# Layer normalisation of the first attention layer moved from VectorE to ScalarE, from the third batch on

## What is computed

```
def _layernorm(x, axis=-1, eps=1e-05):
    m = jnp.mean(x, axis=axis, keepdims=True)
    v = jnp.var(x, axis=axis, keepdims=True)
    return (x - m) / jnp.sqrt(v + eps)
...
    x = x + _L0_attn_a_ref(_layernorm(x, axis=-1), ...)
    x = x + _L0_ffn_ref(_layernorm(x, axis=-1), ...)
    x = x + _L0_attn_b_ref(_layernorm(x, axis=-1), ...)
    x = x + _L0_ffn_ref(_layernorm(x, axis=-1), ...)
```

## Time and profile before

| what | value |
|---|---|
| median of 3 runs | 965.94 us (963.97 to 966.96) |
| the profiled execution's own time | 966.79 us |
| its span, first to last instruction | 965.1 us |
| busy: PE, DVE, ACT, POOL | 890.3, 733.7, 533.5, 381.6 us |
| mean granted TensorE clock | 0.975 |

### The profile page before, as it was taken

One profiled execution on the slowest core, in us unless ns is written; L12 is line 12 of the kernel. 1 busy time (PEld: TensorE's weight loads), 2 busy tenths in 40 slices (PEclk: granted clock), 3 DMA queues, 4 the chain that ended last, 5 costly groups with the idle time before them and its releaser, 6 DMA issues.

```text
span 965.1 us, 20229 instructions
## 1 busy us (share of the span) xinstructions
PE 890.3 (92%) x6766; PEld 696.7 (72%) x6766; DVE 733.7 (76%) x2379; ACT 533.5 (55%) x1410; POOL 381.6 (40%) x554
## 2 busy tenths in 40 slices
PE   5779998989999999978999999999999997999996
PEld 4656776767767776656878888788878776777763
DVE  6668888889889887664766767685867677889973
ACT  6545454543445454526667575757575762554555
POOL 2468788876535443351212112020202000444445
PEclk9789999999999999989999999999999999999999
DMA  6432333331113655001202020202112021132321
GB/s 199 61 54 56 54 45 55 54 55 36 35 35 68 134 109 132 2 16 41 45 1 45 1 44 2 45 2 45 23 23 45 1 34 33 38 62 47 73 48 35
DMA packets 51287, 46.63 MB, mean 48 GB/s; under 512 B 6624, under 2 KB 48624, under 8 KB 51184
## 3 DMA queue, kind: packets, MB, share of 16 engines
q1 hardware_dynamic: 51184, 45.34, 23.4%
HBM read 11.40 MB, written 2.10 MB: 14 GB/s over the span
## 4 chain that ended last, share of the span: by engine, by line
PE 35%; DVE 12%; issue 4%; ACT 1%; DMA 1%; POOL 0%; SPq 0%; POOLq 0%; ACTq 0%; DVEq 0%
PE bank L285 9%; PE bank L1928 5%; PE bank L1878 5%; PE bank L1936 4%; PE bank L1866 3%; DVE weights L1442 3%; DVE q_lo L1422 2%; PE bank L1701 2%; DVE weights L1432 2%; PE bank L1713 2%; DVE arena L1270 1%; PE bank L1698 1%; PE bank L1739 1%; ACT oT L944 1%; DVE rope L1420 1%
## 5 line engine op out<-in xcount | busy, mean ns | idle before, releaser
L1270 DVE TENSOR_REDUCE arena<-bank 128x2 f32<-128x512 f32 (+1 forms) x192 | 128.9, 679 | 27.8 <-PE bank L1701 27.3
L886 ACT ACTIVATE weights<-bank 128x512 f32<-128x512 f32 x144 | 85.7, 596 | 115.4 <-PE bank L1713 114.4
L965 ACT ACTIVATE weights<-weights,neg_max 128x128 f32<-128x128 f32 (+1 forms) x256 | 113.8, 449 | 19.4 <-DVE neg_max L1432 19.4
L1432 DVE CUSTOM_DVE_ANT_0 weights<-bank,arena 128x128 f32<-128x128 f32 (+1 forms) x256 | 80.9, 353 | 56.6 <-PE bank L1928 54.8
L696 POOL TENSOR_SCALAR_AFFINE_SELECT weights<-weights 128x256 f32<-128x256 f32 x144 | 68.3, 475 | 127.4 <-ACT weights L886 127.3
L972 ACT ACTIVATE weights<-bank 128x384 f32<-128x384 f32 x128 | 62.7, 490 | 85.6 <-PE bank L1936 83.4
L1701 PE MATMUL bank<-kf_stack,q_stack 96*128 96x128 f32 (+1 forms) x512 | 109.8, 317 | 0.0
L1928 PE MATMUL bank<-kbT,arena 128*128 128x128 f32 (+1 forms) x512 | 105.1, 328 | 1.1 <-DVE y L420 0.9
L648 POOL TENSOR_SCALAR weights<-weights 128x512 f32<-128x512 f32 x64 | 97.3, 1530 | 13.4 <-ACT weights L789 13.1
L1442 DVE TENSOR_SCALAR weights<-weights,inv_sum 128x128 f32<-128x128 f32 (+1 forms) x256 | 83.8, 370 | 4.5
L285 PE MATMUL bank<-x_hi,wb_hi 128*128 128x256 f32 x256 | 83.4, 326 | 2.8 <-DVE q_lo L1422 2.8
(11 more groups left out here) (232 smaller groups left out, 2412.0 us busy)
## 6 DMA issues: line engine op xcount, KB each, us to landing
q_stack<-q_hi SPq DMA_DIRECT2D x96, 128.0 KB, 3.8
arena<-arena SPq DMA_DIRECT2D x64, 128.0 KB, 2.5
q_stack<-q_lo SPq DMA_DIRECT2D x48, 128.0 KB, 4.0
ka_stack<-k_hi SPq DMA_DIRECT2D x32, 76.5 KB, 3.6
x_all<-x SPq DMA_DIRECT2D x8, 256.0 KB, 5.1
st_wo<-b_wo SPq DMA_DIRECT2D x8, 256.0 KB, 3.9
arena<-b_wqn SPq DMA_DIRECT2D x8, 256.0 KB, 3.4
out<-x_all SPq DMA_DIRECT2D x8, 256.0 KB, 2.1
```

Source lines behind the costliest of these rows:

```text
L886: a.activation(s["pT"][(STEPS * b + k) % N_PT], p2[k % 2][:, :], ACT.Exp).then_inc(s["exp"], 1)
L965: last = a.activation(p, p, ACT.Exp, scale=-1.0, bias=neg_max[:, h % 4, t:t + 1], accum_out=sums[:, h % 4, t:t + 1])
L1270: v.tensor_reduce(into, p1[k % 2][:, :].rearrange("p (h k) -> p h k", h=n), AX.X, ALU.max, negate=True).then_inc(s["maxed"], 1)
L1432: last = v.tensor_tensor_reduce(out=probs[:, h % 4, part], in0=ps_s[h % 2][:, part], in1=mask_b[:, (1 - t) * P:2 * P], scale=1.0, scalar=F ...
```

## The change

From the third batch on (b >= 0, which prepares batches 2 to 7) ACT normalises x in attn_a, at k = 8 and ahead of q_hi, in place of DVE at k = 9. ACT does it in two operations for each half: first x plus the negated mean (Identity with a bias for each token), then, after a wait for its own two results, a product with `rstd` (Copy with a scale for each token), in place in `xn`. POOL writes the negated mean `neg_mean` between the epsilon and the power, in every `pool_rstd`, thus in all four layers. The first two batches of attn_a and all batches of the other layers are still normalised by DVE. The signal `xn` now counts three for a batch in place of one, `rstd` three in place of two, and DVE's statistics and POOL's `pool_rstd` wait for the batch before through `last_of`.

```diff
+        neg_mean = sb("neg_mean", [P, NT])
...
+        def last_of(s, name, b):
+            if s is sa or b > 0:
+                return at(s, name, b, 0)
+            of = sa if s is sf[0] else sf[0] if s is sm else sm
+            return at(of, name, B - 1, of["per"][name])
...
         def dve_stats(s, b):
             v = nc.vector
+            v.wait_ge(*last_of(s, "rstd", b))
...
             g = nc.gpsimd
             wait_apart(g, *at(s, "stats", b, 4))
+            g.wait_ge(*last_of(s, "xn", b))
             g.tensor_scalar(var_eps[:, :], mv[:, :, 1], EPS_LN, None, ALU.add).then_inc(s["rstd"], 1)
-            g.wait_ge(*at(s, "rstd", b, 1))
+            g.tensor_scalar(neg_mean[:, :], mv[:, :, 0], -1.0, None, ALU.mult).then_inc(s["rstd"], 1)
+            g.wait_ge(*at(s, "rstd", b, 2))
             g.tensor_tensor(rstd[:, :], var_eps[:, :], expo[:, :], ALU.pow).then_inc(s["rstd"], 1)
+
+        def act_normalize(s, b):
+            act = nc.scalar
+            act.wait_ge(*at(s, "rstd", b, 3))
+            act.wait_ge(*last_of(s, "xT", b))
+            for t in range(NT):
+                act.activation(xn[:, t, :], x_tile(b, t), ACT.Identity, bias=neg_mean[:, t:t + 1]).then_inc(s["xn"], 1)
+            act.wait_ge(*at(s, "xn", b, NT))
+            for t in range(NT):
+                last = act.activation(xn[:, t, :], xn[:, t, :], ACT.Copy, scale=rstd[:, t:t + 1])
+            last.then_inc(s["xn"], 1)
...
-            nc.tensor.wait_ge(*at(s, "xn", b, 1))
+            nc.tensor.wait_ge(*at(s, "xn", b, NT + 1))
...
+                if k == 8 and b >= 0 and there(b + 2):
+                    act_normalize(sa, b + 2)
                 if k == 8 and there(b + 1):
                     high(b + 1, "q")
...
-                if k == 9 and there(b + 2):
+                if k == 9 and b < 0 and there(b + 2):
                     dve_normalize(sa, b + 2)
```

More of the change, by code:

```diff
@@ L142, in signals @@
         def signals(layer, kind, **own):
-            per = dict(stats=4, rstd=2, xn=1, xT=1, x_hi=1, x_lo=1, x_done=1, **own)
+            per = dict(stats=4, rstd=3, xn=NT + 1, xT=1, x_hi=1, x_lo=1, x_done=1, **own)
             return dict(kind=kind, per=per, past=0, **{n: sem(f"{layer}_{n}") for n in per})
@@ L309, in pool_rstd @@
             wait_apart(g, *at(s, "stats", b, 4))
+            g.wait_ge(*last_of(s, "xn", b))
             g.tensor_scalar(var_eps[:, :], mv[:, :, 1], EPS_LN, None, ALU.add).then_inc(s["rstd"], 1)
-            g.wait_ge(*at(s, "rstd", b, 1))
+            g.tensor_scalar(neg_mean[:, :], mv[:, :, 0], -1.0, None, ALU.mult).then_inc(s["rstd"], 1)
+            g.wait_ge(*at(s, "rstd", b, 2))
             g.tensor_tensor(rstd[:, :], var_eps[:, :], expo[:, :], ALU.pow).then_inc(s["rstd"], 1)
+        def act_normalize(s, b):
[8 more added lines that the diff above has]
+            last.then_inc(s["xn"], 1)
         def dve_normalize(s, b):
             v = nc.vector
[L316 to L320, removed]
+            v.wait_ge(*at(s, "rstd", b, 3))
+            v.wait_ge(*last_of(s, "xT", b))
             for t in range(NT):
-                last = v.tensor_scalar(xn[:, t, :], x_tile(b, t), mv[:, t, 0:1], rstd[:, t:t + 1],
-                                       ALU.subtract, ALU.mult)
-            last.then_inc(s["xn"], 1)
+                v.tensor_scalar(xn[:, t, :], x_tile(b, t), mv[:, t, 0:1], rstd[:, t:t + 1],
+                                ALU.subtract, ALU.mult).then_inc(s["xn"], 1 + t)
         def pe_transpose_x(s, b):
-            nc.tensor.wait_ge(*at(s, "xn", b, 1))
+            nc.tensor.wait_ge(*at(s, "xn", b, NT + 1))
             for c in range(NC):
```

## The result

| | changed kernel | before, in the same comparison |
|---|---|---|
| median | 971.23 us (970.29 to 972.38, 5 runs) | 965.94 us (963.97 to 966.96, 5 runs) |
| ratio | 1.0065, 95% interval 1.0053 to 1.0077 | |
| profiled execution, its span | 972.38 us, 970.6 us | 966.79 us, 965.1 us |

The kernel became slower by 0.65%. The forecast of 967.7 us and its likeliest case (966.0 to 969.3) were too low by 3.5 us and by 1.9 us; only the wide range of 962 to 973 holds the result. "Same" had the largest chance; the result lies above the forecast's own bound of 968.8 for "slower".

A forecast was written before the change was run, and what follows sets the result against it. The prediction took a loop through DVE, ACT, POOL's chain and PE to bound the first layer. With +1.8 us on POOL and nothing on DVE and ACT, 965.94 us became 967.7 us, with a wide range of 962 to 973.

The forecast's parts named there:

- likeliest case: Whole kernel: the summed terms hold, 966.0 to 969.3 us with the spread of the runs; chance 0.67.
- Same: Whole kernel: no change that can be told, between 963.0 and 968.8 us; chance 0.66.
- slower: Whole kernel: a median above 968.8 us; chance 0.20.
- other rivals: First layer: ACT late, 974.3 us (0.14); PE the bound, 959 us (0.05); PE's clock staying up, some 962 us (0.09).
- What bounds the kernel: First layer: a 27.25 us loop through DVE, ACT, POOL and PE, with DVE's normalisation outside it.
- Part 1: DVE, six iterations: two operations leave, 1.3 to 2.8 us of DVE time each, worth nothing because ACT's results wait for POOL.
- Part 2: POOL: neg_mean ahead of the power adds 0.30 us in six iterations, 1.8 us; nothing in the other 26 uses.
- Part 3: ACT before q_hi: four operations and a wait, 1.8 to 2.2 us, cost nothing within a 2.66 us gap.
- The sign named for it: ACT in the later profile: q_hi still waits for POOL's sum, some 3.5 us in place of 5.5.
- The clock stays down for longer: PE, first layer: a second half-level stretch in five iterations costs 5 us more, 973 us; chance 0.05.

The follow-up runs named there:

- e8: Kernel before, with DVE's statistics half an iteration earlier and POOL's epsilon and power ahead of k_lo, in POOL's wait for k_hi: 960.11 us, ratio 0.9947.
- e1: Kernel before plus neg_mean on POOL in all 32 uses, read by nothing, DVE still normalising: 967.36 us, ratio 1.0022.
- e2: Changed kernel with neg_mean made only for the six batches that ACT normalises: 970.16 us, ratio 1.0051 to the kernel before.
- e9: Changed kernel with DVE's statistics earlier and POOL's epsilon, neg_mean and power ahead of k_lo: 956.78 us, ratio 0.9915 to the kernel before.
- e12: Changed kernel run once more with no edit: 971.93 us, ratio 1.0068 to the kernel before.
- e3: Changed kernel with neg_mean made by ACT for its six batches, and not by POOL at all: 968.23 us, ratio 1.0030 to the kernel before.
- e5: Changed kernel in which DVE also normalises, into a spare tile that nobody reads: 970.60 us, ratio 1.0048 to the kernel before.
- e7: Changed kernel with three more unread products on PE, in its idle time before the transposed scores: 970.22 us, ratio 1.0042 to the kernel before.
- e4: Changed kernel with DVE's f_lo in iteration 2 held until after POOL's sum: 970.37 us, ratio 1.0052 to the kernel before.
- e11: Changed kernel with ACT normalising only the last three batches, neg_mean still in all 32 places: 970.22 us, ratio 1.0047 to the kernel before.
- e6: Kernel before plus neg_mean on POOL and ACT's four operations into a spare tile, DVE still normalising: 968.63 us, ratio 1.0040.

## Why the prediction was off

The mechanism that the forecast named, neg_mean in POOL's chain, is there, but its term was mis-sized: 1.8 us in place of 2.7. Two costs that it put at nothing came on top, POOL's sum held up by f_lo (some 1 us) and a part that goes with the clock (1 to 2 us, by correlation only). The range of 962 to 973 holds the result because it was drawn wide for other rivals, and not by the sum. The likeliest case's own range doesn't quite follow from the terms given for it either: 965.94 + 0.7 and + 1.9, with 0.1% either way, make 965.7 to 968.8. By its steps:

**What bounds the kernel.** The loop over POOL's chain stood up: e8 took 5.94 us out of the chain and got 5.7 us back. DVE's normalisation is not in the loop: PE starts its transposes 2.25 us behind q_hi with and without it.

**Part 1, "Its worth by the argument above is nothing".** Right for PE: the wait of 1.46 us before the scores became one of 2.47 us before the transposed scores. But the step took no port time lost for POOL, "0 to 0.1 us for an iteration in POOL's favour", and the sign was wrong. DVE without its work reached f_lo early and held POOL's sum for 0.8 us. In the first trace a small operation is stretched in one more iteration (neg_mean 0.51 us at b = 1). Together they are 1.0 to 1.2 us (3.67 and 3.88 against e1's 2.70). That the two POOL rows were equal showed nothing on this: beside them stood DVE's normalisation, and what harms POOL is another DVE instruction, which came earlier.

**Part 2, "6 x 0.30 = 1.8 us".** This is the term that was mis-sized. neg_mean does add 0.3 us, but var_eps ahead of it starts 0.1 us later than before and in three of the six iterations lasts some 0.5 us or more in place of 0.22. Measured by itself it is 2.70 us in the segments, and 1.9 us between medians. The loop, forecast at 27.5 us, is 27.3 in iteration b = 5 by the starts of q_hi (153.40 to 180.71); it was 27.18 by the same starts before. What shows the loss is the segment, since the rest of an iteration moves by more than the term. That the 26 other uses cost nothing was right within 1 us (e2), and in the trace the changed kernel's lag behind the kernel before, by the starts of PE's transposes of xn, is 5.67 us at 449 us and 5.51 us at 912 us, so the fourteen uses of neg_mean between those two points added none.

**Part 3, "Cost 0 while the gap holds".** Right. Each pair took 0.91 us, all four 1.85 us with the wait between them, inside the 1.8 to 2.2 us forecast; q_hi still waited 0.80 us for POOL. The sign named for it, that q_hi waits some 3.5 us for POOL's sum, did not follow from the forecast's own numbers: a gap of 2.66 us less 1.8 to 2.2 us of work leaves 0.5 to 0.9. The 3.43 us stand before the normalisation. e9 settles it from the other side.

**The rival "The clock stays down for longer".** It had 0.05 and a price of 5 us, for a second stretch in five iterations. That did not come: the iterations b = 2 to 5 have one stretch each in both traces. But there is more time at the lower level. It is 54.4 us (five runs) and 56.4 us (e12's six) against 50.6. At 0.28 us for each that makes 1.1 to 1.6 us.

**The account.** 3.88 us in the segments and 1.1 us by the clock make 5.0 us for the first comparison, 3.67 and 1.6 make 5.3 us for e12; measured were 5.3 and 6.2. The same two terms, the column of the segments plus 0.28 times the change of the lower-level time, give every kernel of the table within 1.3 us of the difference of its mean from that of before (965.64 over all 68 executions): e3 0.7 + 1.6 = 2.3, measured 2.8; e9 -5.6 - 3.2 = -8.7, measured -8.4; the worst are e5, e7 and e12, which the sum puts 1.1 to 1.3 us too low.

**What stays open.** Why there is more time at the lower level is not known. The kernels in which DVE doesn't write xn in those iterations (the changed one, e2, e3, e4, e11) have 54.4 to 57.1 us, those in which it does (before, e1, e5, e6) 50.2 to 52.6. In the former PE stands still once for 2.47 us at b = 5, in the latter for 1.46 us with a head's scores before the next wait, and this looks like the cause. The traces speak mostly against it: in the first one the iterations b = 2 to 5 have the same time at the lower level as before, and the excess lies elsewhere; in e12's only one iteration has more (b = 2, some 7 us in place of 3.4). That work in the idle time (e7, 46.7) or a shorter idle time (e9, 0.75 us of it, 39.3) goes with less time at the lower level shows that such stretches can be avoided, not that the change made more of them. Nor is the price of the clock sure: the profiled executions of the changed kernel in the first comparison and in e12 took 972.38 us both, at granted clocks of 0.967 and 0.973, 64.2 and 52.5 us at the lower level. So 1 to 2 us of the loss have no cause that an experiment shows; a cost of ACT's operations through PE's wait is a rival that e6 leaves room for. And why an operation behind it makes var_eps begin 0.1 us later no run tells.

## What to carry to other kernels

Before work is moved from a busy engine to an idle one, write down which engine's chain closes the loop, and count every instruction that the move puts into that chain, however small: here one operation of 0.23 us cost 2.7 us over six iterations, while the pair that left DVE, 2.76 us in one iteration, gave nothing. The gap of the idle engine tells what it waits for, and the gain lies in that chain: POOL's small operations, moved to where POOL waits anyway, gave 5.7 us, and only then was the change itself free. Price a small operation by what its neighbours on the other engines do at the new moment, not by its duration alone.

## What was not expected of the hardware

- An operation of 128x2 on POOL lasted 0.22 us or 0.50 us by what DVE did beside it. In the changed kernel var_eps starts at 176.41 and DVE's 128x512 operation L1111 at 176.44, 0.03 us later, and var_eps ends at 176.91, just behind the end of L1111. Before, it had started at 172.39 and DVE's operation only at 172.53, just ahead of its end:

```profile
172.53 0.42 DVE L1088 TENSOR_SCALAR arena<-arena 128x512 f32<-128x512 f32 x1
```

So a shift of a tenth of a microsecond decided here whether DVE's operation met var_eps or, for its last part, only the power behind it, which then took 0.83 us in place of 0.72.
- DVE's subtraction with two inputs in SBUF took 1.24 us when it started ahead of POOL's q_lo, and 2.27 us when it started 0.14 us behind POOL's product; POOL's sum, next in line, took 2.10 us in place of 1.28. One meeting cost both engines, DVE 1.0 us and then POOL 0.8.
- ACT's operations with one operand for each token were steadier than DVE's that they replaced. In the changed kernel, duration ns min/median/max:

```profile
L333 ACT ACTIVATE xn<-x_all,neg_mean x12: 493/501/509, 43.8 to 178.5; 128x256 f32<-128x256 f32 x12
L336 ACT ACTIVATE xn<-xn,rstd x12: 492/501/512, 44.8 to 179.4; 128x256 f32<-128x256 f32 x12
```

The Trainium skill, ScalarE: Activation LUTs, section "What ACT_TABLE_LOAD costs", gives 280 ns plus 0.833 ns for each element with a bias by pointer, and the same price for each pointer operand, so also for a scale. For 256 elements that is an estimate of 493 ns. The rows agree within 2%; DVE's took 392 to 1494 ns.
- Executions of one kernel on one chip spread by up to 10 us (e4: 965.31 to 975.52), and the granted clock went with them, from 0.977 to 0.965. With twelve runs the intervals here are still 2.2 to 4 us wide, so a difference of 1 us between two kernels is not resolved by them, and a single trace may lie on either side.
